# Attention scores as two one-pass products of rounded parts and rests, and router logits as extra columns of the value and output projections

## The reference

```python
h = _L0_tok_ref(x, ...)                      # patches @ W + b, class token, + pos_embed
h = jnp.concatenate([h, txt], axis=1)
h = h + _L0_attn_ref(_layernorm(h), Wq, bq, Wk, bk, Wv, bv, Wo, bo)
...
q, k, v = rope(X @ Wq + bq), rope(X @ Wk + bk), X @ Wv + bv
scores = einsum('bqhd,bkhd->bhqk', qh, kh) / sqrt(hd)       # masked, softmax
out = einsum('bhqk,bkhd->bqhd', weights, vh).reshape(B, S, D); return out @ Wo + bo
...
pc = softmax(h @ Wsc + bsc); route_c = argmax(pc)           # "common" experts, with a capacity
pu = softmax(h @ Wsu + bsu); route_u = argmax(pu)           # "unique" experts
out = common + dropped * unique
```

## Time and profile before

| | |
|---|---|
| median of 3 runs | 1395.81 us (1387.93 to 1400.01) |
| span of the profiled execution | 1318.5 us |
| its own time | not listed; taken as the span and 77.3 us around it |
| PE, DVE, ACT, POOL busy | 91%, 67%, 42%, 47% of the span |
| granted clock of PE over the span | 0.969 of full speed |
| attention stage | to about 900 us |

### The profile page before, as it was taken

The page is one execution under the profiler, slowest core; times in us unless marked ns, Lnnn a source line. Parts: engine busy times, 40 slices in busy tenths (PEclk is TensorE's granted clock), DMA queues, the critical chain, the costliest instruction groups (busy, mean ns, idle before and its releaser), DMA issues. The chain is left out here.

```text
span 1318.5 us, 33201 instructions
## 1 busy us (share of the span) xinstructions
PE 1196.7 (91%) x12722; PEld 1019.6 (77%) x12722; DVE 887.9 (67%) x1991; ACT 555.8 (42%) x959; POOL 622.7 (47%) x990
## 2 busy tenths in 40 slices
PE   5899999999999999999999999883899999999993
PEld 4667777777777777777777777663899899999993
DVE  5667677767777678678767777746897755545441
ACT  1234434444444433443443444441544455555550
POOL 4133333333543453444444454443452477775565
PEclk8899999999999999999999999995999999999997
DMA  6001121113321331232223221237887678987651
GB/s 212 28 23 42 43 70 49 42 47 93 105 62 58 106 100 61 81 119 68 81 77 103 80 80 37 92 95 249 287 279 253 191 253 262 308 259 267 219 185 35
DMA packets 84367, 168.03 MB, mean 127 GB/s; under 512 B 16446, under 2 KB 57701, under 8 KB 84208
## 3 DMA queue, kind: packets, MB, share of 16 engines
q1 hardware_dynamic: 70544, 139.88, 33.5%
q0 software_dynamic: 13664, 26.00, 5.5%
HBM read 123.83 MB, written 45.45 MB: 128 GB/s over the span
## 5 line engine op out<-in xcount | busy, mean ns | idle before, releaser
L759 ACT ACTIVATE PT<-round_banks 128x1752 f32<-128x1752 f32 x96 | 156.6, 1632 | 173.0 <-PE round_banks L591 173.0
L876 POOL TENSOR_SCALAR_AFFINE_SELECT PT<-PT 128x512 f32<-128x512 f32 x192 | 118.1, 640 | 208.9 <-ACT PT L759 208.4
L1765 ACT ACTIVATE Gl<-h_ps,W 128x256 f32<-128x256 f32 x264 | 115.5, 474 | 172.0 <-PE h_ps L1675 164.0
L1686 PE MATMUL y_ps<-W,Gl 128*128 128x192 f32 x1056 | 181.2, 325 | 0.0
L1686 PEld LDWEIGHTS y_ps<-W,Gl 128*128 128x128 f32 x1056 | 171.3, 189 | 0.0
L1675 PE MATMUL h_ps<-XH,Wh 128*128 128x256 f32 x528 | 147.5, 297 | 10.0 <-DVE Wl L1834 6.9
L511 PE MATMUL gen<-w_emb,xT 128*128 128x192 f32 (+1 forms) x768 | 141.8, 336 | 7.4 <-DMA ident<-in_ident_dram 7.4
L1675 PE MATMUL h_ps<-XH,Wl 128*128 128x256 f32 x528 | 140.1, 286 | 0.0
L994 DVE TENSOR_TENSOR capped<-round_banks,masks_f 128x1024 f32<-128x1024 f32 x96 | 116.3, 1211 | 32.7 <-PE round_banks L564 32.2
L511 PEld LDWEIGHTS gen<-w_emb,xT 128*128 128x128 f32 (+1 forms) x768 | 118.1, 170 | 15.6 <-DMA ident<-in_ident_dram 7.4
L591 PEld LDWEIGHTS round_banks<-QKT 32*128 32x128 f32 x2304 | 94.5, 186 | 42.6 <-DVE nm L996 23.0
(11 more groups left out here) (273 smaller groups left out, 2445.5 us busy)
## 6 DMA issues: line engine op xcount, KB each, us to landing
W<-in_experts_dram SPq DMA_DIRECT2D x44, 771.0 KB, 5.1
W<-in_experts_dram SPq DMA_DIRECT2D x44, 672.0 KB
xT<-in_xT_dram SPq DMA_DIRECT2D x32, 591.0 KB, 4.3
X<-sorted_d SPq DMA_DIRECT2D x35, 386.0 KB, 5.6
stage<-rows_d SPq DMA_DIRECT2D x64, 192.0 KB
rows_d<-h SPq DMA_DIRECT2D x32, 192.0 KB
out_dram<-h SPq DMA_DIRECT2D x32, 192.0 KB
rows_d<-xn SPq DMA_DIRECT2D x32, 192.0 KB
```

The costliest lines, as they stand in the source:

```text
L759: act.activation(PT[(JG * b + j) % 2][:], R[:, :, 0:438], ACT.Exp, scale=SCALE).then_inc(exps, 1)
L876: pool.affine_select(x[:, :, at:at + P], x[:, :, at:at + P], [[0, GH], [1, P]], ALU.is_ge, 0.0, base=0, channel_multiplier=-1)
L1686: mm = pe.matmul(y_ps[t.par][:, k * D:(k + 1) * D], Gl[t.par][:, f, k * P:(k + 1) * P], W[t.i][:, W2O + f * D:W2O + (f + 1) * D], start=(f ...
L1765: act.activation(Gl[t.par][:, f, :], h_ps[f % 3][:, 0:ROWS], ACT.Gelu, bias=W[t.i][:, B1O + f:B1O + f + 1]).then_inc(g_ready, 1)
```

## The change

So the product of a rounded q with this mix and that of a rest with a rounded k make up the score; each f32 product of `maxs` and `scores` becomes two such products. ACT rounds the heads (`copy_heads`), DVE forms the rests (`rest_heads`, `rest_tails`). The maxima, too, are laid as two rows, the rounded part and the rest, which DVE forms (`mT` has two planes). The tail maxima stay f32, with q from a tile `Qt`. V has 17 columns a head and not 32.

The logits are linear in h, so the router weights are folded into the value and output projections as eight extra columns (`w_qkv`, `w_o`; the folding is done on the chip in the first turns: `sum_router`, `fold_router`). ACT scales the part that comes from the token itself by its standard deviation, which POOL makes (`root_std`), DVE adds the part from the output projection and finishes with rstd and bias (`add_scores`, `finish_scores`). X2, X2t, RT and RTt fall away. On PE `values(t.fin, 1)` now stands ahead of `maxs(t.mid, 0)`.

```diff
-          ("KQt0", "1"), ("KQt1", "1"), ("X2", 5), ("V1", 1), ("PV0", 3), ("XTt", "0"), ("ATt", "8"), ("RTt", "10"), ("UTt", "7"),
-          ("AT", 4), ("RT", 5), ("RK", "12"), ("QKt", "0"), ("X2t", "9"), ("KQ0", 1), ("KQ1", 1), ("MT", 2), ("Vt", "0"), ("KQ2", 1), ("WO", 4),
+          ("KQt0", "1"), ("KQt1", "1"), ("V1", 1), ("PV0", 3), ("XTt", "0"), ("ATt", "8"), ("UTt", "7"),
+          ("AT", 4), ("RK", "12"), ("QKt", "0"), ("KQ0", 1), ("KQ1", 1), ("MT", 2), ("Vt", "0"), ("KQ2", 1), ("WO", 4),
           ("WOt", "8")]
 ROUNDS = [("M0", 2), ("S0", 3), ("M1", 2), ("S1", 3), ("M2", 2), ("T", 2), ("S2", 3)]
...
-                    q = QKT[b % 3]
-                    for j in range(JG):
-                        for k in range(2):
-                            sp.dma_start(q[HD:P:SLOT, j, tok(k)], mT[12 * j + 2 * k:12 * j + 12:3, :]).then_inc(mrow_in[b % 2], 16)
-                    sp.dma_start(q[HD:P:SLOT, 0:JG, 2 * P:S],
-                                 mT[36:40, 0:JG * SLOT].rearrange("i (j r) -> i j r", r=SLOT)[:, :, 0:TL]).then_inc(mrow_in[b % 2], 16)
+                    for w in range(2):
+                        q, m = HX[b % 3][HD + w:P:SLOT, 1].bitcast(F32), mT[:, w, :].bitcast(F32)
+                        for j in range(JG):
+                            for k in range(2):
+                                sp.dma_start(q[:, j, tok(k)], m[12 * j + 2 * k:12 * j + 12:3, :]).then_inc(mrow_in[b % 2], 16)
+                        sp.dma_start(q[:, 0:JG, 2 * P:S],
+                                     m[36:40, 0:JG * SLOT].rearrange("i (j r) -> i j r", r=SLOT)[:, :, 0:TL]).then_inc(mrow_in[b % 2], 16)
...
-                q = QKT[b % 3]
+                hi, lo = HX[b % 3][:, 0], HX[b % 3][:, 1]
                 for k, at in ((1, P), (0, 0)):
-                    for i in range(GH):
-                        rows = slice(SLOT * i, SLOT * (i + 1))
-                        mm = pe.matmul(R[:, i, at:at + (k + 1) * P], q[rows, j, tok(k)], q[rows, JG + j, 0:(k + 1) * P],
-                                       start=True, stop=True, skip_group_check=True)
+                    keys = slice(0, (k + 1) * P)
+                    for q, x, n, first in ((hi, lo, SLOT, True), (lo, hi, HD, False)):
+                        for i in range(GH):
+                            rows = slice(SLOT * i, SLOT * i + n)
+                            mm = pe.matmul(R[:, i, at:at + (k + 1) * P], q[rows, j, tok(k)], x[rows, JG + j, keys],
+                                           start=first, stop=not first, skip_group_check=True)
                 mm.then_inc(r_filled, 1)
 
             def maxs_tail(b):
 
...
-                    pe.wait_ge(mrow_in[b % 2], 112 * (b // 2 + 1))
+                    pe.wait_ge(mrow_in[b % 2], 224 * (b // 2 + 1))
                 fill_round(f"S{j}", b)
-                q, o = QKT[b % 3], SLOT * (b % 4)
+                hi, lo, o = HX[b % 3][:, 0], HX[b % 3][:, 1], SLOT * (b % 4)
                 for klo, qlo, n, at in ((0, 0, S, 0), (P, P, S - P, S), (2 * P - o, 2 * P, TL, 2 * S - P)):
-                    for i in range(GH):
-                        rows = slice(SLOT * i, SLOT * (i + 1))
-                        mm = pe.matmul(R[:, i, at:at + n], q[rows, JG + j, klo:klo + P], q[rows, j, qlo:qlo + n],
-                                       start=True, stop=True, skip_group_check=True)
+                    m = min(P, KW - klo)
+                    for x, q, deep, first in ((lo, hi, SLOT, True), (hi, lo, HD + 2, False)):
+                        for i in range(GH):
+                            rows = slice(SLOT * i, SLOT * i + deep)
+                            mm = pe.matmul(R[0:m, i, at:at + n], x[rows, JG + j, klo:klo + m], q[rows, j, qlo:qlo + n],
+                                           start=first, stop=not first, skip_group_check=True)
                 mm.then_inc(r_filled, 1)
 
             def values(b, j):
...
+                if t.fin is not None:
+                    values(t.fin, 1)
                 if t.mid is not None:
                     for c in range(3):
                         have(f"KQ{c}", t.mid)
                     maxs(t.mid, 0)
                 if t.fin is not None:
-                    values(t.fin, 1)
...
+                if k == 0:
+                    act.wait_ge(std_ready, i + 1)
+                col = UNIT * (i // 4) + 2 * (i % 4) + k
+                act.activation(by_token[:, col, :], g[:, D:DV], ACT.Copy, scale=std[:, i % 2, k:k + 1]).then_inc(scores_in, 1)
...
-                g = take(f"KQ{c}", b)
-                emptied(f"KQ{c}", b, act.activation(QKT[b % 3][:, 2 * c:2 * c + 2, 0:2 * P],
-                                                    g[:].rearrange("p (j t) -> p j t", j=2), ACT.Copy))
+
+                g = take(f"KQ{c}", b)[:].rearrange("p (j t) -> p j t", j=2)
+                for lo, hi in ((0, 1), (1, 2)) if c == 1 else ((0, 2),):
+                    dst, src = HX[b % 3][:, 0, 2 * c + lo:2 * c + hi, 0:2 * P], g[:, lo:hi, :]
+                    if 2 * c + lo < JG:
+                        ins = act.activation(dst, src, ACT.Copy)
+                    else:
+                        ins = act.activation(dst, src, ACT.Identity, scale=keep, bias=unit)
+                ins.then_inc(heads_rounded, 1)
...
-                    emptied("MT", t.mid, act.activation(mT[:], g[:, 0:P], ACT.Copy))
+                    act.activation(mT[:, 0, :], g[:, 0:P], ACT.Copy).then_inc(m_rounded, 1)
...
-                                   ropeB[:, k, :].rearrange("p (h d) -> p h d", d=HD), ALU.add).then_inc(rr_ready, 1)
+                                   ropeB[:, k, :].rearrange("p (h d) -> p h d", d=HD), ALU.add).then_inc(rr_added, 1)
+                pool.wait_ge(rr_added, 2 * b + k + 1)
+                pool.tensor_copy(rr[:, k, :, HD:SLOT], rr[:, k, :, 0:HD]).then_inc(rr_ready, 1)
...
-                    pool.tensor_copy(QKT[b % 3][:, :, 2 * P:S], QKTt[:, :, lanes(b)]).then_inc(tails_copied, 1)
+                    pool.tensor_copy(HX[b % 3][:, :, :, 2 * P:S], HXt[:, :, :, b % 4, :].bitcast(F32)).then_inc(tails_copied, 1)
...
+            def rest(dst, hi, g):
+
+                return dve.scalar_tensor_tensor(dst, hi.bitcast(F32), low, g, ALU.mult, ALU.add)
+
+            def rest_heads(b, c):
+                g = take(f"KQ{c}", b)[:].rearrange("p (j t) -> p j t", j=2)
+                dve.wait_ge(heads_rounded, JG * b + c + 1)
+                js = slice(2 * c, 2 * c + 2)
+                emptied(f"KQ{c}", b, rest(HX[b % 3][:, 1, js, 0:2 * P], HX[b % 3][:, 0, js, 0:2 * P], g))
+
+            def rest_tails(g):
+                for use, lo, hi, n in (("KQt0", 0, 4, 2), ("KQt1", 4, 6, 3)):
+                    src = take(use, g)[:, 0:(hi - lo) * P].rearrange("p (j t) -> p j t", t=SLOT)[:, :, 0:TL]
+                    dve.wait_ge(tails_rounded, 3 * g + n)
+                    flat_j = lambda x: x[:, lo:hi].rearrange("p j q t -> p (j q) t")
+                    emptied(use, g, rest(flat_j(HXt[:, 1]), flat_j(HXt[:, 0]), src))
+
             def stats(which, k, x):
...
+            def col_of(b):
+                return UNIT * (b // 4) + 2 * (b % 4)
+
+            def add_scores(x, more):
+
+                nonlocal added
+                added += 1
+                dve.tensor_tensor(x, more, x, ALU.add).then_inc(scores_added, 1)
+
+            def finish_scores(x, by):
+
+                nonlocal finished
+                finished += 1
+                dve.wait_ge(scores_added, added)
+                dve.scalar_tensor_tensor(x, x, by, w_r[:, 2, :], ALU.mult, ALU.add).then_inc(scores_done, 1)
 
             def norm_tail(g):
                 dve.wait_ge(tail_in[g % 4], 64 * (g // 4 + 1))
...
-                    x = h[b % 8][:].rearrange("p t d -> p (t d)")
-                    emptied("WO", b, dve.tensor_tensor(x, g[:, 0:2 * D], x, ALU.add))
+                    o = g[:, 0:2 * DV].rearrange("p (t d) -> p t d", d=DV)
+                    dve.wait_ge(scores_in, 2 * b + 2 + b // 4 + 1)
+                    add_scores(by_token[:, col_of(b):col_of(b) + 2, :], o[:, :, D:DV])
+                    x = h[b % 8][:]
+                    emptied("WO", b, dve.tensor_tensor(x, o[:, :, 0:D], x, ALU.add))
...
+                if t.pre is not None:
+                    rest_heads(t.pre, 0)
+                    rest_heads(t.pre, 1)
+                if t.mid is not None:
+                    g = take("MT", t.mid)
+                    dve.wait_ge(m_rounded, t.mid + 1)
+                    emptied("MT", t.mid, dve.tensor_tensor(mT[:, 1, :], g[:, 0:P], mT[:, 0, :].bitcast(F32), ALU.subtract))
...
+                if t.pre is not None:
+                    rest_heads(t.pre, 2)
```

204 lines of the change are left out of this document (119 added, 85 removed).

## The result

The changed kernel takes 1517.46 us (median of five runs, 1509.20 to 1520.20), the kernel before 1395.79 on the same chip (1387.93 to 1400.01). The ratio is 1.096, with a 95% interval from 1.091 to 1.101. The profiled execution took 1509.20 us and has a span of 1507.4 us, so only 1.8 us lie around a span.

The account below looks back on a forecast made before the run. A loop through DVE's minima, SP's row DMAs and the next scores group was to overtake PE: 2.4 us a turn, 74 us over 31 turns, plus 40 clock, minus 5 at the end, on 1395.8: 1505 us, range 1440 to 1570.

Parts of the forecast that it names:

- Fourteen issues: SP's row-maxima DMAs: 14 issues where there were 7, one behind the other, add 3.9 us a turn before the last lands.
- Before the first issue: DVE's rests and subtraction ahead of the row DMAs: the first issue comes 1.0 us a turn later, 2.6 us when routes are chosen.
- What was to spare: Slack of the row-maxima loop against PE's turn, mean 2.8 us, taken off the added time of each turn.
- The idle piece: PE ahead of the scores group: 7 us of work against 10.9 us of waiting, so 4 us idle in one piece.
- The scores group: 24 score matmuls on PE, 1.06 us before: could lose 0.37 us, 0.3 taken off the loop; groups near 0.7 us.
- rival C: One-pass products no faster below 256 columns: loop 0.3 us a turn longer, 1514 us; chance 0.58 together with the forecast.
- The clock: PE's clock falls after waiting for the rows: 1.3 us lost a turn, 40 us in all; 102 if the whole piece ran low.
- POOL: POOL's extra copies of rotated halves and tails delay the tail maxima: 0.6 us a turn, between 0 and 1.2.
- PE's relief: Scores, router matmuls, transposes and tails give PE back 3.3 us a turn; only the scores group counts, the rest becomes waiting.
- Rival A: PE sets the pace and rows arrive in time: turns of 23.4 us, 93 us less, 1300 us; chance 0.12.
- Start and end: Router work falling away at the stage's end gains 5 us; the start changes by nothing that can be priced, within 3 us.
- The 77.3 us: Difference between the earlier kernel's median, 1395.8 us, and its profiled span, 1318.5 us, taken to lie around the span.

Follow-up runs that it names:

- the first two experiments: The changed kernel laying only the rounded row of maxima by seven DMAs, ratio 1.035; the changed kernel laying both rows by six DMAs, ratio 1.034.
- the first experiment: The run e1: the changed kernel without the seven DMAs of the maxima's rests; ratio 1.035 to the kernel before.
- e0: The kernel before, run again without edits for a second profile: 1387.27 us for a span of 1385.5; 807.7 us for 31 turns.
- e1: The changed kernel with only the rounded row's seven DMAs, the rest not subtracted from the scores: 841.2 us for 31 turns, ratio 1.035 to the kernel before.
- e10: The changed kernel with one rounded row, its bank freed by ACT, no DVE subtraction, DVE's work reordered: 807.8 us for 31 turns, ratio 1.011 to the kernel before.
- e9: The kernel before with only the router logits as extra columns, scores left in f32: 793.7 us for 31 turns, ratio 0.997.

## Why the prediction was right

1505 us were forecast and 1517.5 measured; the mechanism was the one described, and the first two experiments show it: without eight or seven of the issues 73 us of the loss are gone. That the total came so close is in part luck. In the turns 3.7 us each were forecast and 3.44 measured, but POOL's 0.6 us and 0.2 of those before the first issue didn't come, and 0.7 us came instead because less slack was used up than was taken off. Outside the turns, 5 us of gain were forecast and some 15 of loss measured. Term by term, with means over 29 turns that I worked out from the time lines of both kernels:

- **Fourteen issues.** From first to last issue 7.23 us and not 3.30: 3.93, forecast 3.9. The landing is 1.65 us (rows of SP and PE above).
- **Before the first issue.** 3.08 and not 2.29 us: 0.8, forecast 1.0. The turn with the choice gained 2.5 (forecast 2.6).
- **What was to spare.** Last issue to scores was 4.45 us and is 2.34. 2.1 were used up and not 2.8: in the turns with tails the scores group is held by late PE work, not by rows, so that slack never came in. Not foreseen; it is what the first experiment uncovers.
- **The idle piece.** 4 us were forecast, from 7 us of PE work against 10.9 of waiting. The 10.8 us are there (499.55 to 510.34), but PE works for 7.7 of them and waits 0.8 us elsewhere, so that the piece ahead of the group is 2.2 to 2.8 us in ordinary turns. This is one reason why PE's share in the turns is 84% and not the 75% forecast.
- **The scores group.** 0.81 us (482.82 to 483.63) against 1.06; forecast near 0.7. The one-pass products are faster below 256 columns too, which ends rival C.
- **The clock.** The stretch from scores to second embedding is 4.22 us and was 3.78; at full clock it is 3.4 (3.44 in the rows above). So 0.8 us a turn are lost in that piece, 24 us in 31 turns. Forecast 1.3 and 40 us, for that piece. The low clock reaches beyond it, and over whole ordinary turns the mean (the turns from 270 to 917 us) lies 1.3 and 1.5 us above the turns of the same kind at full clock (26.6 and 27.4 us); the turns with tails or a choice have none at full clock to compare with. So the size was about right, but partly for work that the forecast didn't count. The section of the Trainium skill cited there (TensorE: Matmul & The Clock Gate, HAM oscillation) has the fall in each pass; the windows at 511 to 514 agree for a wait of 2.26 us, but the turn at 423.42 waits 2.81 us and goes through at full clock. Of 17 groups that waited 2.06 to 2.81 us for their rows the clock fell behind 11 and not behind 6, and 102 us by that rule would have been far too much.
- **POOL.** This step was wrong, though its 0.6 us a turn did little harm. The tail maxima of `t.mid` need the copy that POOL made a turn earlier (`tails_copied` reaches `b + 1` then), so POOL's extra copies can't hold them. The 0.37 us that the earlier trace rows put down to POOL were a wrong attribution. In the kernel after, PE starts them at 497.02, released by DVE, ahead of the copy that the profile would have named:

```profile
497.24 0.36 POOL L965 CAST HX<-HXt 128x216 fp32r<-128x216 f32 x1
```

- **PE's relief** turned into waiting, as said; that it could not have been cashed in was only half seen. Rival A put a turn without row waits at 23.4 us. The kernels with one row have ordinary turns of 24.3 to 25.6 us: DVE's 12.4 us from embedding to minima and the way back, 11.9 us at the least, follow each other in every turn and can't overlap.
- **Start and end.** The start is 5.8 us later (forecast within 3): the first maxima, at 38.69 us before, start at 44.00 after, since PE waits 1.91 us for the folded router weights and works at low clock; with the router part alone it is 3.2 us later. At the end 5 us were to fall away; 7.3 came on top. The last turn's first scores group waits 3.06 us for its rows (at 989.32). The router part alone makes this stretch 3.7 us longer and not shorter, so the forecast gain there had the wrong sign; I haven't traced through what.
- **The 77.3 us** around the span don't exist. The execution of the earlier trace rows had an expert stage 65 us shorter than that of e0. The forecast survived since it added a difference, made of turns, to the median.

By the runs, the 106.6 us in the turns split so: 73 us go with the second seven issues (e1); 33 more with DVE's order, its subtraction and the bank that DVE frees, which weren't told apart (e10 against e1); about 14 are gained by the router part (e9), and the same amount is lost by what is left of the scores (e10 ends where the kernel before was). The last is a difference of two runs and not shown by one of its own.
